# Local attention: the mask is added by VectorE as it copies the scores to SBUF

## What is computed

```python
# 16 heads of 64, windows of w = 32; each window sees itself and the one before
q, k = l2norm(q) * qs, l2norm(k) * ksc          # then rotated by position
mask = (it < jb) | (it > jb + w) | (jb == -1)
sim = jnp.einsum('bhwie,bhwje->bhwij', bq, bk2) * 8.0
sim = jnp.where(mask, -jnp.finfo(sim.dtype).max, sim)
attn = jax.nn.softmax(sim, -1)
out = jnp.einsum('bhwij,bhwje->bhwie', attn, bv2)
```

## Time and profile before

| | |
|---|---|
| Median of 3 runs | 4206.79 us (4199.53 to 4208.95) |
| Profiled execution | 4219.19 us |
| Its span | 4217.4 us |
| TensorE busy | 3722.3 us (88%) |
| VectorE busy | 2758.5 us (65%) |
| ScalarE busy | 2221.3 us (53%) |
| GpSimd busy | 1398.7 us (33%) |
| Mean granted TensorE clock | 0.932 |

### The profile page before, as it was taken

The page is one execution under the profiler, slowest core; times in us unless marked ns, Lnnn a source line. Parts: engine busy times, 40 slices in busy tenths (PEclk is TensorE's granted clock), DMA queues, the critical chain, the costliest instruction groups (busy, mean ns, idle before and its releaser), DMA issues. The chain is left out here.

```text
span 4217.4 us, 100218 instructions
## 1 busy us (share of the span) xinstructions
PE 3722.3 (88%) x40681; PEld 2007.5 (48%) x40681; DVE 2758.5 (65%) x4886; ACT 2221.3 (53%) x4121; POOL 1398.7 (33%) x621
## 2 busy tenths in 40 slices
PE   7979778888859977999999999999899976998998
PEld 3344333333334434666666666666666642334335
DVE  5943457777633357787778778778787747773335
ACT  3323236777723335767676676666667623552222
POOL 3710022111100005666666666666666510000000
PEclk9979868999969988999999999999999987997999
DMA  1000037776520002322322322322222202000000
GB/s 50 0 1 0 0 112 238 232 231 225 177 86 0 0 0 49 98 60 57 95 57 62 95 57 63 93 58 71 81 62 62 52 28 79 20 23 1 0 0 11
DMA packets 168634, 283.54 MB, mean 67 GB/s; under 512 B 36253, under 2 KB 71424, under 8 KB 165736
## 3 DMA queue, kind: packets, MB, share of 16 engines
q1 hardware_dynamic: 167900, 276.87, 22.3%
q10 hardware_dynamic: 268, 0.19, 0.0%
HBM read 101.95 MB, written 74.45 MB: 42 GB/s over the span
## 5 line engine op out<-in xcount | busy, mean ns | idle before, releaser
L2183 POOL TENSOR_TENSOR b2f_norm<-b2f_norm,b2f_minus_half 128x16 f32<-128x16 f32 x192 | 555.1, 2911 | 277.1 <-DVE b2f_norm L2524 277.1
L2173 POOL TENSOR_TENSOR b2f_q<-b2f_q,b2f_q_part 128x1024 f32<-128x1024 f32 x96 | 228.1, 2376 | 850.9 <-DVE b2f_q_part L2514 850.9
L1621 ACT ACTIVATE b1a_weights<-b1a_b_ps 128x512 f32<-128x512 f32 x512 | 277.4, 597 | 39.8 <-PE b1a_b_ps L1546 37.8
L1728 DVE TENSOR_REDUCE b1a_tops<-b1a_a_ps 128x1 f32<-128x512 f32 (+3 forms) x512 | 244.4, 501 | 19.6 <-PE b1a_a_ps L1502 18.1
L1621 ACT ACTIVATE b3a_weights<-b3a_b_ps 128x512 f32<-128x512 f32 (+3 forms) x384 | 161.5, 503 | 161.6 <-PE b3a_b_ps L1556 161.5
L2523 DVE TENSOR_REDUCE b2f_norm<-xn 128x16 f32<-128x1024 f32 x192 | 234.2, 1220 | 13.6 <-ACT xn L2407 6.5
L2466 ACT ACTIVATE b2f_v_rows<-b2f_q_ps 128x1024 f32<-128x1024 f32 x96 | 98.3, 1023 | 270.1 <-DMA b2f_values<-b2f_v_rows 142.6
L2416 ACT ACTIVATE b2f_prob<-b2f_odd_ps,b2f_bias,b2f_norm 128x64 f32<-128x64 f32 x768 | 232.0, 445 | 13.5 <-DVE b2f_bias L2540 12.4
L1707 DVE TENSOR_REDUCE b3a_tops<-b3a_a_ps 128x1 f32<-128x512 f32 (+3 forms) x384 | 194.7, 553 | 67.9 <-PE b3a_a_ps L1502 65.7
L1445 POOL TENSOR_SCALAR b1a_k_op<-b1a_k_op,b1a_extra 128x1024 bf16<-128x1024 bf16 x32 | 90.6, 2842 | 433.4 <-DMA b1a_k_op<-part_copies 433.4
L2416 ACT ACTIVATE b2f_prob<-b2f_even_ps,b2f_bias,b2f_norm 128x64 f32<-128x64 f32 x768 | 231.9, 450 | 2.3 <-DVE b2f_bias L2540 2.3
(11 more groups left out here) (484 smaller groups left out, 8499.4 us busy)
## 6 DMA issues: line engine op xcount, KB each, us to landing
b2f_values<-b2f_v_rows SPq DMA_DIRECT2D x1534, 64.0 KB
position_scratch<-b1a_e_sb SPq DMA_DIRECT2D x128, 512.0 KB, 3.9
b1a_band<-position_scratch SPq DMA_DIRECT2D x128, 384.0 KB
b2f_wqkv<-in_b2f_wqkv SPq DMA_DIRECT2D x6, 1536.0 KB, 7.1
b2f_turn<-in_c_rotary SPq DMA_DIRECT2D x6, 1024.0 KB, 8.2
part_copies<-b1a_parts SPq DMA_DIRECT2D x12, 256.0 KB
b2f_wo<-in_b2f_wo SPq DMA_DIRECT2D x6, 512.0 KB, 9.5
part_copies<-b3a_parts SPq DMA_DIRECT2D x12, 256.0 KB
```

The source lines that it names most:

```text
L1621: act.activation(weights[:, s % P_RING, c, lo:QW], b_room(s, c)[:, lo:QW], ACT.Exp).then_inc(S.exps_ready, 1)
L1728: ins = dve.tensor_reduce(out, src, AX_X, ALU.max)
L2173: pool.tensor_tensor(G.q[:, g % 2], G.q[:, g % 2], G.q_part[:], ALU.add) \
L2183: pool.tensor_tensor(part, part, G.minus_half[:, 0:HEADS], ALU.pow) \
```

## The change

`scores` no longer writes the mask. Each small score product now starts its own sum. VectorE adds the mask to the 128x1024 scores while it moves them from PSUM into a new SBUF tile `masked`. `maxima` and `exps` read `masked`. The turn of the keys waits for that copy instead of the exponentials. The mask pattern stays a bf16 tile in SBUF, broadcast over the heads.

```diff
@@ scores
-                unseen = G.mask[:, 0 if g % QT == 0 else 1].unsqueeze(1).to_broadcast([P, PAIRS, HD2])
-                for h in range(2):
-                    pe.matmul(ps[:, h], G.ident16[:], unseen, start=True, stop=False,
-                              skip_group_check=True)
...
-                                            start=False, stop=True, skip_group_check=True)
+                                            start=True, stop=True)
@@ TensorE's queue, ahead of the turn of the keys
-                        pe.wait_ge(S.exps_done, HEADS * (s - 1))
+                        pe.wait_ge(S.masked, s - 1)
@@ exps
-                    act.activation(G.prob[:, i // 2, i % 2], ps[:, i % 2, cols(i // 2, HD2)], ACT.Exp,
+                    act.activation(G.prob[:, i // 2, i % 2], G.masked[:, PAIRS * (i % 2) + i // 2], ACT.Exp,
@@ maxima
+                unseen = G.mask[:, 0 if g % QT == 0 else 1].unsqueeze(1).to_broadcast([P, HEADS, HD2])
+                dve.tensor_tensor(G.masked[:], ps[:].rearrange("t h n -> t (h n)").rearrange(
+                    "t (k j) -> t k j", j=HD2), unseen, ALU.add).then_inc(S.masked, 1)
+                dve.wait_ge(S.masked, g + 1)
                 chain(dve.tensor_reduce(G.top[:].rearrange("t (p h) -> t h p", h=2),
-                                        ps[:].rearrange("t h (p j) -> t h p j", j=HD2), AX_X, ALU.max))
+                                        G.masked[:].rearrange("t (h p) j -> t h p j", h=2), AX_X, ALU.max))
```

More of the change, by code:

```diff
@@ L2074, in block2_ffn @@
             qt=one("qt", PAIRS, P), kt=one("kt", PAIRS, WIN + P),
-            prob=one("prob", PAIRS, 2, HD2), pt=one("pt", PAIRS, P),
+            masked=one("masked", HEADS, HD2), prob=one("prob", PAIRS, 2, HD2), pt=one("pt", PAIRS, P),
             top=one("top", HEADS), bias=one("bias", HEADS), total=one("total", PAIRS, 2),
@@ L2118, in layers_of_attention @@
                "summed", "inverted", "k_normed", "kt_turned", "qt_turned", "kt_copied", "qt_copied",
-               "carried", "v_ready", "v_copied", "scores_ready", "bias_ready", "exps_done", "totalled",
+               "carried", "v_ready", "v_copied", "scores_ready", "masked", "bias_ready", "exps_done", "totalled",
                "probs_turned", "pt_copied", "out_ready", "o_scaled", "o_turned", "o_copied", "y_ready",
@@ L2408, in square, with exps @@
                                ACT.Square).then_inc(S.squared, 1)
-            def exps(g, ps):
+            def exps(g):
                 act.wait_ge(S.bias_ready, g + 1)
@@ L2469, in _ @@
                 if 0 <= s - 1 < n_tiles:
-                    exps(s - 1, here)
+                    exps(s - 1)
                 ffn(s, 0)
```

## The result

Over 8 runs of each, the changed kernel has a median of 4177.11 us (4162.26 to 4188.7), the kernel before 4203.46 us (4189.91 to 4209.3). The ratio is 0.994, with a 95% interval of 0.9921 to 0.9958: 25 us faster, 18 to 33. The forecast was 4164 us and a saving of 43 us, so the direction and the range hold, and the forecast saving is 1.7 times the measured one.

What follows compares the result with a forecast made beforehand. TensorE, 94% busy, was taken as the bound, with a ScalarE-VectorE loop close behind in the short step. 1.9 us per four-step cycle over 22.5 cycles, opening and drain cancelling, saves 43 us: 4164 us, range 4146 to 4210.

Steps and rivals of the forecast that it cites:

- TensorE's saving: Two mask products leave TensorE's queue in each tile: 0.53 us for both, 51 us over 96 tiles.
- second long step: One of two long steps (18.8 and 18.1 us) in each four; far from ScalarE and VectorE's limit, each gains 0.53 us.
- the loop: ScalarE-VectorE round from output copy through maxima, bias and 16 exponentials to the next copy: 13.8 us, becoming 15.4.
- short step: Third step of four (feed-forward phase 2), 15.65 us between output copies: becomes 15.4, set by the loop, gaining 0.2 to 0.3.
- VectorE's add: VectorE adds the mask to the 128x1024 scores: 1.27 us per tile, 122 us in all, fitting into VectorE's waits.
- rival that VectorE becomes the bound: The 1.27 us exposed in every step, costing 0.74 us x 96, +71 us: slower, 4276 us at full price; chance 0.15.
- gate steps: Fourth step of four (phase 3), score products standing behind three gate products: each gains 0.53 + 0.2 us.
- The exponentials: The 16 per tile read SBUF instead of PSUM: +20 ns each, 0.32 us per tile, range 0 to 0.56.
- The end of the stage: The drain after the last steps, where the ScalarE-VectorE chain is exposed: gives back about 2 us.
- cycle: Four steps repeating with the feed-forward phases: gains 3 x 0.53 + 0.25 + 0.2 - 0.15 = 1.9 us, 43 us over 22.5.
- absorbed 0.2 us in the gate step: TensorE's wait there for the values' copy, behind DMAs, makes good about 0.2 us of what the short step lost.
- waits behind the gate step: 22 output-copy waits, 0.43 to 6.81 us, hide 1.6 us of lateness; four under 1.3 us lose about 0.15 us per cycle.

Runs made afterwards that it cites:

- no_mask: The kernel before without its 192 mask products and nothing in their place, the mask left out of the computation: 4170.47 us, ratio 0.9931.
- both: The changed kernel with the two mask products per tile kept as well: 4202.95 us, ratio 1.0009 to the kernel before.
- in_place: The changed kernel, but VectorE adds the mask inside PSUM, maxima and exponentials read PSUM, and the keys' turn waits for the exponentials: 4165.39 us, ratio 0.9917.
- add_psum_exps: The changed kernel, but exponentials read unmasked PSUM scores and the keys' turn waits for them again: 4165.21 us, ratio 0.9914.
- split order: Four kernels with the gate step's value products moved ahead of its gate products; ratios: before 0.9931, no mask 0.9852, mask added in place 0.9953, the change 0.9994.
- sbuf_exps: The kernel before, but the 16 exponentials of a tile read a constant SBUF tile of zeros: 4200.47 us, ratio 1.0004.

## Why the prediction came out as it did

- **TensorE's saving: the term that was mis-sized.** I priced the masks at 0.53 us, from their start to the next start. The handoff between the neighbours that are left costs 0.10 us more, so it is 0.43 us, 41 us and not 51. Of these 29 arrive, with and without the additions (`no_mask`; `both` against the change). The second long step and, without the loop's new work, the short step show about the 0.43. Where the other 12 us go, the runs do not say: two traces with the same TensorE work differ by as much. That part stays open.
- **VectorE's add**: 1224 ns, as forecast, and hidden, as forecast (`in_place`, `add_psum_exps`). The rival that VectorE becomes the bound was wrong for this order of work. In the split order the add is exposed, but in the gate steps and those behind them and not in every step: 42 us, where the rival had 122 us of adds exposed against 51 saved (its 4276 should read 4278, 4206.79 + 71).
- **The exponentials: the second mis-sized term.** 16 take 5.41 us and not 4.83, +0.58 us, where the sum had +0.32 and its upper bound 0.56. I had chosen +20 ns per instruction from the wide form with an operand; the +35 of the narrow form would have been nearer. Both were durations, though, and here the duration of one fell (445 to 427 ns) while the distance from one to the next grew, so that the +35 fits may be luck. The Trainium skill's 43 ns (VectorE: DVE Perf Modes, on the TRN2 errata) was nearer than the 20; measured are 36. In the order of before it is hidden (`sbuf_exps`), with the add in the loop it costs about 10 us, most of it in the short steps.
- **The loop**: right. 13.8 + 1.27 + 0.58 = 15.65 us against the 15.56 in the trace and a short step of 15.65 before. So the short step gains nothing, where I had put 0.25 us; the means over 21 of them, 15.95 and 15.92, agree. The 15.65 that I read was one of the shortest, the median before is 15.8.
- **The end of the stage.** From the third-last output copy to the last it takes 3.7 us longer after the change, where I had 2:

```profile
3379.04 1.02 ACT L2445 ACTIVATE b2f_o_cols<-b2f_even_ps 128x1024 f32<-128x1024 f32 x1 [4.57 <-PE b2f_even_ps L2251]
...
3405.03 1.02 ACT L2445 ACTIVATE b2f_o_cols<-b2f_even_ps 128x1024 f32<-128x1024 f32 x1 [2.50 <-PE b2f_even_ps L2251]
```

```profile
3331.75 1.02 ACT L2441 ACTIVATE b2f_o_cols<-b2f_even_ps 128x1024 f32<-128x1024 f32 x1 [2.72 <-PE b2f_even_ps L2251]
...
3361.43 1.02 ACT L2441 ACTIVATE b2f_o_cols<-b2f_even_ps 128x1024 f32<-128x1024 f32 x1 [2.50 <-PE b2f_even_ps L2251]
```

With the measured terms the working of the forecast gives 2 x 0.43 in the long steps, 0 in the short one, 0.43 + 0.2 in the gate step, and 0.20 lost behind it: 1.3 us a cycle, 29 us, less 3.7 at the end and nothing in the opening. That is 25 us, and 25 are measured. The table of steps agrees roughly: against `sbuf_exps` the change gains 0.5 in the gate step, 0.3 behind it, 0.4 in the second long step and nothing in the short one. The mechanism stands, but that the number fits so well is in part luck: the traces scatter by more than the terms, and the absorbed 0.2 us in the gate step was never measured by itself.
- **Right for the wrong reason**: I took the waits behind the gate step as free cover. The larger part of them, 2.29 of 3.26 us, was a stall of TensorE, and the rest TensorE work behind the scores, the value products for one. The add was seen to be free only in that order and with that stall.

## What to carry to other kernels

Price removed matmuls by the distance between the neighbours that are left, not by their own duration or start. Before you hide work behind an engine's wait, ask what makes the wait: if it is a stall, or an order that someone may change, the hidden work can come back, here 42 us when both went. And put a mask where no chain is waiting: after the exponentials, on the least busy engine, an operation of nearly twice the length cost nothing that could be measured.

## What the runs showed of the hardware

The duration that the trace gives for one exponential fell from 445 to 427 ns with the source in SBUF, while the distance between two rose from 302 to 338 ns (4.83/16 and 5.41/16). So for this run of short ScalarE instructions the merged row of the timeline gives the price, and the mean of one does not. An add of PSUM and SBUF takes VectorE about as long into PSUM, in place, as into SBUF: 1232 against 1224 ns. And 256 small matmuls (32 x 64 outputs) in one piece stall TensorE by 2.3 us in the mean of the 22 gate steps, in their second half. With 128x512 products between the halves 1.6 of 51.8 us of these waits are left, while the first half still stalls now and then (11.8 us over 9 times). The place of the stall moves with the count of TensorE's instructions.
